# Evictions, clips and low parts in another order, a residual in transposing form, and a normalisation by single tiles at the end of an expert MLP kernel

## The reference

```python
q, k, v = x @ Wq, x @ Wk, x @ Wv
attn_out = softmax(q @ k.T * 512**-0.5) @ v @ Wp + bp
cms_out = gelu(attn_out @ cW1 + cb1) @ cW2 + cb2 + one_hot(code)
modifier = gelu(concat(attn_out, cms_out) @ mW1 + mb1) @ mW2 + mb2
x = clip(x + cms_out + modifier, 0, 1)                       # layer 0
h = gelu(x @ W_down[e] + b_down[e]) @ W_up[e] + b_up[e]      # layer 1, e per sequence
h = x + h
out = (h - mean(h)) * rsqrt(var(h) + 1e-5) * ln_w[e] + ln_b[e]
```

## Time and profile before

| | |
|---|---|
| three runs | 1076.14, 1076.20, 1076.23 us, median 1076.2 |
| the profiled execution | 1076.12 us, of which the span of the trace is 1074.3 us |
| PE busy | 1048.7 us, 98% of the span |
| DVE busy | 797.5 us, 74% |
| ACT busy | 516.6 us, 48% |
| granted clock of PE | 0.998 of full speed over the span |
| end of the last matmul, of the last DVE instruction | 1066.4 us, 1071.8 us |

### The profile page before, as it was taken

One profiled execution on the slowest core, in us unless ns is written; L12 is line 12 of the kernel. 1 busy time (PEld: TensorE's weight loads), 2 busy tenths in 40 slices (PEclk: granted clock), 3 DMA queues, 4 the chain that ended last, 5 costly groups with the idle time before them and its releaser, 6 DMA issues. The chain is left out here.

```text
span 1074.3 us, 13987 instructions
## 1 busy us (share of the span) xinstructions
PE 1048.7 (98%) x4986; PEld 874.4 (81%) x4986; DVE 797.5 (74%) x1394; ACT 516.6 (48%) x933; POOL 6.4 (1%) x15
## 2 busy tenths in 40 slices
PE   8999999999999999999999999999999999999997
PEld 7889778888877788888889877888887778888876
DVE  4436886776588888877675788677658888878786
ACT  4426755444264543433575485444425554343365
POOL 0000000000000000000000000000000000000001
PEclk9999999999999999999999999999999999999999
DMA  5600121210143242312753122312013323342152
GB/s 195 238 2 20 60 78 40 77 41 20 60 157 117 80 156 79 105 53 78 275 177 98 51 70 79 118 40 79 20 59 129 126 98 121 115 138 68 43 145 79
DMA packets 54718, 101.61 MB, mean 95 GB/s; under 512 B 3102, under 2 KB 31866, under 8 KB 50810
## 3 DMA queue, kind: packets, MB, share of 16 engines
q1 hardware_dynamic: 54560, 100.70, 27.0%
q10 hardware_dynamic: 90, 0.02, 0.0%
HBM read 79.74 MB, written 20.97 MB: 94 GB/s over the span
## 5 line engine op out<-in xcount | busy, mean ns | idle before, releaser
L1076 DVE TENSOR_TENSOR acc<-bank,acc 128x512 f32<-128x512 f32 x224 | 153.9, 687 | 84.9 <-PE bank L223 84.7
L221 PE MATMUL bank<-hid_hi,w_lo 128*128 128x512 f32 x512 | 200.5, 392 | 7.6 <-DVE hid_lo L965 4.7
L645 ACT ACTIVATE sbc<-sbc,bias 128x512 f32<-128x512 f32 x112 | 80.8, 724 | 254.8 <-DVE sbc L1046 193.4
L222 PE MATMUL bank<-hid_hi,w_hi 128*128 128x512 f32 x512 | 199.3, 389 | 0.0
L223 PE MATMUL bank<-hid_lo,w_hi 128*128 128x512 f32 x512 | 199.3, 389 | 0.0
L221 PE MATMUL bank<-ta_hi,w_lo 128*128 128x512 f32 x448 | 175.4, 392 | 2.5 <-ACT sbc L566 1.2
L223 PE MATMUL bank<-ta_lo,w_hi 128*128 128x512 f32 x448 | 174.4, 389 | 0.0
L222 PE MATMUL bank<-ta_hi,w_hi 128*128 128x512 f32 x448 | 174.3, 389 | 0.0
L1046 DVE TENSOR_TENSOR sbc<-bank,sbc 128x512 f32<-128x512 f32 x144 | 98.1, 686 | 42.6 <-PE bank L223 42.4
L221 PEld LDWEIGHTS bank<-hid_hi,w_lo 128*128 128x128 f32 x512 | 96.1, 188 | 31.8 <-DVE w_lo L965 3.6
L223 PEld LDWEIGHTS bank<-hid_lo,w_hi 128*128 128x128 f32 x512 | 96.1, 188 | 20.0
(11 more groups left out here) (223 smaller groups left out, 1556.4 us busy)
## 6 DMA issues: line engine op xcount, KB each, us to landing
w_raw<-in_L_cond_mW SPq DMA_DIRECT2D x48, 512.0 KB, 3.4
w_raw<-in_L_cond_cW SPq DMA_DIRECT2D x32, 512.0 KB, 4.3
pre_d<-sbc SPq DMA_DIRECT2D x10, 1024.0 KB, 3.9
sbc<-pre_d SPq DMA_DIRECT2D x10, 1024.0 KB, 7.2
x_raw<-in_x SPq DMA_DIRECT2D x4, 1024.0 KB, 6.2
e_raw<-in_L_cond_W_down SPq DMA_DIRECT2D x8, 512.0 KB, 5.2
e_raw<-in_L_cond_W_up SPq DMA_DIRECT2D x8, 512.0 KB, 4.4
out<-acc SPq DMA_DIRECT2D x16, 256.0 KB, 2.1
```

The lines of the kernel that those rows point to most:

```text
L221: nc.tensor.matmul(dst, w_l, a_h, start=start, stop=False, **kw)
L222: nc.tensor.matmul(dst, w_h, a_h, start=False, stop=False, **kw)
L645: nc.scalar.activation(dst, dst, ACT.Gelu, **kw).then_inc(g_done[key], 1)
L1076: nc.vector.tensor_tensor(dst, bank[:, :], dst, ALU.add).then_inc(evac, 1)
```

## The change

Four edits.

**The last round on DVE.** A new `dve_mlp_end` takes the last round of the last batch. Each of the four evictions of pair 2 is followed by the clip of its tile; each of the evictions 4 to 6, of pair 3, is followed by one low part of pair 2, and the fourth low part stands ahead of eviction 7. Pieces 4 and 5 (`e0l`) no longer stand among the evictions: piece 4 comes behind the clips of pair 3, and piece 5 behind the low parts of pair 3 (`dve_expert_last`).

The diff, cut to its core:

```diff
@@ pe_up
                     nc.tensor.matmul(ps[b0 + t][:, k * P:(k + 1) * P],
                                      acc[:, k, pp * TB + t * P:pp * TB + (t + 1) * P], ident[:, :],
-                                     start=k == 0, stop=True, skip_group_check=True)
+                                     is_transpose=True, start=k == 0, stop=True, skip_group_check=True)
@@ act_stats
+        A_STAT = ((0, 2), (0, 3), (1, 0), (1, 1), (1, 2))
+        def act_stats(act):
+            for c, (pp, t) in enumerate(A_STAT):
+                col = slice(TT * pp + t, TT * pp + t + 1)
+                bank = ps[(0 if pp else 4) + t][:, :]
+                act.wait_ge(up_mm, 4 * (2 * NBAT - 2 + pp) + t + 1)
...
@@ dve_norm_last
+            for t in (2, 3):
+                dve_eps_last(dve, 0, t)
+                dve_cent_last(dve, 0, t)
+                dve_out_last(dve, 0, t)
+            dve.wait_ge(z_done[0], 4 * bb + 4)
+            dve.wait_ge(ln_in[1], 64 * NBAT)
+            for t in (0, 1):
+                dve_eps_last(dve, 1, t)
+                dve_cent_last(dve, 1, t)
+                dve_out_last(dve, 1, t)
+            for t in (3, 2):
+                dve_eps_last(dve, 1, t)
+            for t in (2, 3):
+                dve_cent_last(dve, 1, t)
+            for t in (2, 3):
+                dve_out_last(dve, 1, t)
@@ the last round
+        def dve_mlp_end(dve, b):
+            i = QB - 1
+            dve_evac(dve, b, i - 1, 7)
+            dve_hid(dve, b, i, "12")
+            for k in range(KT):
+                dve_evac(dve, b, i, k)
+                dve_clip(dve, 2 * b, (k,))
+            for k in range(KT - 1):
+                dve_evac(dve, b, i, KT + k)
+                dve_xp(dve, 2 * b, (k,))
+            dve_xp(dve, 2 * b, (KT - 1,))
+            dve_evac(dve, b, i, 2 * KT - 1)
+            dve_clip(dve, 2 * b + 1)
+            dve_expert_piece(dve, b, 4)
@@ dve_expert_last
-            for k in (2, 3):
+            for k in (5, 2, 3):
                 dve_expert_piece(dve, bb, k)
...
-            dve_norm(dve, 2 * bb)
+            dve_norm(dve, 2 * bb, (0,))
```

More of the change, by code:

```diff
@@ L944, in act_expert_last @@
             act_up_bias(act, 2 * bb + 1)
[L945 to L956, removed]
+            act_stats(act)
+        A_STAT = ((0, 2), (0, 3), (1, 0), (1, 1), (1, 2))
+        A_NO = {pt: c for c, pt in enumerate(A_STAT)}
+        def act_stats(act):
[3 more added lines that the diff above has]
+                act.wait_ge(up_mm, 4 * (2 * NBAT - 2 + pp) + t + 1)
+                nc.scalar.activation(sjunk[:, c, 0, :], bank, ACT.Identity, accum_out=ssum[:, col]).then_inc(sum_done, 1)
+                act.wait_ge(sum_done, c + 1)
+                nc.scalar.activation(nmean[:, col], ssum[:, col], ACT.Copy, scale=-1.0 / V).then_inc(nmean_done, 1)
+                act.wait_ge(nmean_done, c + 1)
+                nc.scalar.activation(sjunk[:, c, 1, :], bank, ACT.Square, bias=nmean[:, col],
+                                     accum_out=ssq[:, col]).then_inc(ssq_done, 1)
         def act_program(act):
@@ L1118, in dve_resid, with dve_clip @@
             nc.vector.tensor_tensor(dst, dst, xf[:, t, :, :], ALU.add).then_inc(resid_done, 1)
-        def dve_clip(dve, n):
+        def dve_clip(dve, n, tiles=range(4)):
             b, t = divmod(n, 2)
-            for j in range(KT):
+            for j in tiles:
                 dve.wait_ge(evac, 8 * (RB * b + RB - 1) + KT * t + j + 1)
@@ L1165, in dve_expert_piece, with dve_xp @@
             sub(lo[:, s, :], e_raw[E_STAGE[bb][k]][:, s, :], hi[:, s, :]).then_inc(e_l, 1)
-        def dve_xp(dve, n):
+        def dve_xp(dve, n, tiles=range(4)):
             pp = n % 2
-            for j in range(KT):
+            for j in tiles:
                 dve.wait_ge(xp_h, 4 * n + j + 1)
@@ L1205, in dve_norm @@
                         .then_inc(z_done[pp], 1)
-        def dve_norm_last(dve):
[L1208 to L1225, removed]
@@ new lines, in build, with dve_eps_last @@
+        R_TILE = ((0, 2), (0, 3), (1, 0), (1, 1), (1, 3), (1, 2))
+        R_NO = {pt: 4 * NBAT - 3 + c + 1 for c, pt in enumerate(R_TILE)}
+        def dve_eps_last(dve, pp, t):
+            one = slice(t, t + 1)
+            if (pp, t) in A_NO:
+                col = slice(TT * pp + t, TT * pp + t + 1)
+                dve.wait_ge(ssq_done, A_NO[(pp, t)] + 1)
+                nc.vector.tensor_scalar(veps[:, one], ssq[:, col], 1.0 / V, LN_EPS, ALU.mult, ALU.add).then_inc(ve_done, 1)
+            else:
+                dve.wait_ge(up_mm, 8 * NBAT)
+                nc.vector.bn_stats(stat[:, t, :], ps[t][:, :]).then_inc(st_done, 1)
+                dve.wait_ge(st_done, 8 * NBAT - 5)
+                nc.vector.bn_aggr(mv[:, t, :], stat[:, t, :]).then_inc(ag_done, 1)
+                dve.wait_ge(ag_done, 8 * NBAT - 5)
+                nc.vector.tensor_scalar_add(veps[:, one], mv[:, t, 1:2], LN_EPS).then_inc(ve_done, 1)
@@ new lines, in dve_cent_last @@
+        def dve_cent_last(dve, pp, t):
+            n = 2 * NBAT - 2 + pp
+            mean = nmean[:, TT * pp + t:TT * pp + t + 1] if (pp, t) in A_NO else mv[:, t, 0:1]
+            nc.vector.scalar_tensor_tensor(out=z_tile(pp, t), in0=ps[(0 if pp else 4) + t][:, :], scalar=mean,
+                                           in1=ln_p[n][:, t // TS, 0, :],
+                                           op0=ALU.add if (pp, t) in A_NO else ALU.subtract, op1=ALU.mult)\
+                .then_inc(z_cent, 1)
@@ new lines, in dve_out_last @@
+        def dve_out_last(dve, pp, t):
+            n = 2 * NBAT - 2 + pp
+            dve.wait_ge(rstd_done, R_NO[(pp, t)])
+            dve.wait_ge(z_cent, 4 * n + t + 1)
+            nc.vector.scalar_tensor_tensor(out=z_tile(pp, t), in0=z_tile(pp, t), scalar=rstd[:, t:t + 1],
+                                           in1=ln_p[n][:, t // TS, 1, :], op0=ALU.mult, op1=ALU.add)\
+                .then_inc(z_done[pp], 1)
+        def dve_norm_last(dve):
+            bb = NBAT - 1
+            for t in (2, 3):
[14 more added lines that the diff above has]
+                dve_out_last(dve, 1, t)
@@ L1419, in dve_mlp @@
                 if it >= QB and b + 1 == NBAT:
-                    dve_expert_piece(dve, b, 1 if it == QB else 5)
-                last = it == QB + 1 and b + 1 == NBAT
+                    dve_expert_piece(dve, b, 1)
                 turn = it == QB + 1 and b + 1 < NBAT
-                if last:
-                    dve_clip(dve, 2 * b)
                 down(4)
@@ L1437, in dve_mlp @@
                 down(6)
[L1438 to L1441, removed]
+            dve_clip(dve, 2 * b)
             dve_evac(dve, b, QB - 1, 7)
@@ L1470, in pool_program @@
             pool.wait_ge(consts, 1)
+            halves = [slice(2 * h, 2 * h + 2) for h in range(2)]
+            singles = [slice(t, t + 1) for t in range(TT)]
             for n in range(NB):
-                for h in range(2):
-                    part = slice(2 * h, 2 * h + 2)
-                    pool.wait_ge(ve_done, 2 * n + h + 1)
+                last = (halves[0], singles[2], singles[3]) if n == NB - 2 else tuple(singles[t] for t in (0, 1, 3, 2))
+                for c, part in enumerate(halves if n < NB - 2 else last):
+                    pool.wait_ge(ve_done, (2 * n if n < NB - 1 else 2 * NB - 1) + c + 1)
                     nc.gpsimd.tensor_tensor(rstd[:, part], veps[:, part], mhalf[:, part], ALU.pow).then_inc(rstd_done, 1)
```

13 lines of the change are left out of this document (8 added, 5 removed).

## The result

| | before | after |
|---|---|---|
| median (lowest to highest) | 1076.22 us (1076.14 to 1076.48, 4 runs) | 1065.78 us (1065.63 to 1065.96, 4 runs) |
| ratio, 95% interval | | 0.9902, 0.989 to 0.9913 |
| the profiled execution, its span | 1076.12, 1074.3 us | 1065.9, 1064.0 us |
| granted clock of PE over the span | 0.998 | 0.999 |
| end of the last matmul, of the last DVE instruction | 1066.39, 1071.78 us | 1056.65, 1061.44 us |

The kernel is 10.4 us faster. 3.05 were forecast: 1073.1 us, in a range from 1072.1 to 1074.7. The first table of the page of after, to be read against the earlier trace rows, says where to look: PE has 64 instructions fewer (4986 before) and 8.7 us less to do (1048.7 before), though no edit takes a product out of the program.

What follows compares the result with a forecast made beforehand. PE, busy for 98% of the span, was taken to bound the kernel. Terms of -2.3, -0.7, +0.5, -0.3 and -0.25 sum to -3.05 us against 1076.12, giving 1073.1 us; 8-in-10 range 1072.1 to 1074.7.

Steps and rivals of the forecast that it cites:

- (4): Residual's matmuls in transposing form on PE: slightly smaller spacing per instruction, 0.3 us gained in all, between 0 and 0.34.
- (1): Last round: with DVE's new order no group waits for DVE and `pe_down` starts at 1033.6; 2.3 us gained.
- (2): First 12 matmuls of `pe_down`: pair 2's low parts are ready in time, so no waiting; 0.7 us gained.
- (3): Pair 3's down product: PE waits for the moved piece 5; 0.5 us lost, bounds 0 and 1.0.
- (5): Tail behind PE's last matmul: single-tile normalisation with statistics on ACT and DVE, 5.39 to 5.15 us; 0.25 us gained.
- A: Rival: DVE falls behind in the interleaved last round and holds PE, losing 1.5 us of gain; 1074.6 us, chance 0.13.
- B: Rival: single tiles in the tail cost more than they save, each unit waiting for POOL; 1073.9 us, chance 0.08.
- D: Rival: DVE's pieces come before PE wants them and POOL's one-column power takes half; 1072.1 us, chance 0.07.
- C: Rival: PE's clock falls during 32 transposes, slowing the up products behind them; 1078.5 us, chance 0.05.

Runs made afterwards that it cites:

- e1: Kernel before with only the transposing flag on the residual's 64 matmuls; 1068.65 us, ratio 0.9931.
- e2: Changed kernel with the residual's flag taken back, so plain matmuls again; 1073.39 us, ratio 0.9972.
- e5: Kernel before, residual of pairs 2 and 3 as plain product on fp32r operands, without bias and low part; 1072.93 us, ratio 0.9966.
- e6: Kernel before with the 32 transposes of the attention weights as plain float32 products with the identity; 1079.69 us, ratio 1.0031.
- e7: Kernel before with the transposing flag on the residual of pairs 2 and 3 only; 1072.6 us, ratio 0.9963.
- e3: Kernel before with only the last round's new order on DVE, pieces 4 and 5 moved behind the evictions; 1073.61 us, ratio 0.9976.
- e4: Kernel before with only the normalisation edits: single tiles, statistics on two engines; 1075.54 us, ratio 0.9993.
- e0: Changed kernel run once more, unaltered; 1065.68 us.
- e9: Changed kernel with POOL making piece 4's low part only behind pair 2's clips, DVE making piece 5 behind pair 3's clips; 1066.53 us.
- e8: Changed kernel with POOL instead of DVE making the low parts of pieces 4 and 5, right behind their high parts; 1067.2 us.

## Why the prediction was wrong, point by point

**(4), the transposing form, is the term that failed.** It was put at 0.3 us and measured at 7.1 to 7.7. The step took the spacing of one instruction of each form (0.109 and 0.112 us, both right) and multiplied their difference by the rows' 32, as if the form could change only the duration of one and not how many there are. Sixteen products at 2 x 0.109 us before (3.49/32), 16 at 0.104 (1.66/16) after: the price of a product halved. The prediction's own sign for this step was a row of L449 x32 of 3.66 us; the trace has x16 of 1.91. It could have been read without a run. The earlier trace rows show x32 for L449 and x16 for L360; the text of the kernel has 4 x 4 products in the one and 4 x 4 transposes in the other. The section on the kernel even says "32 float32 matmuls of 128 columns a pair", which is the count of the trace put in place of that of the code. e1 (one line, 7.7 us), e2 (3.0 us without it), e5 (fp32r, no flag, the same 16 instructions) and e6 (the reverse, 3.4 us slower) show that the count is the cause. Of the two places each gives its half (e7).

The Trainium skill's page "FP8 and Floating Point Precision", section "TensorE Precision Notes", says that true float32 takes four passes through the array. The trace shows two instructions for a product in place of one; how many passes each makes no run here shows. By that rule a factor would have been asked of the flag rather than a difference: as an estimate from the page, and if the transposing form takes a single pass, three quarters of 3.49 us for each of four pairs, 10.5 us. The trace shows about half, 7.3.

**(1) and (2)** came to 0.02 us as forecast, and e3 alone gives them. **(3)**, the new wait for piece 5, was 0.47 by the adding up and 0.44 in the trace, released by `e0l` as named, 7.5 us behind the first matmul of `pe_down` (forecast 7.4); the row's idle time alone is 0.17, less than the 0.3 to 0.4 named as the sign, and the slow start is the rest.

**(5), the tail, was right in its mechanism and too small**: 0.60 us for 0.25. The duration for a power on one column, taken at 0.69 for want of a row, is 0.55. Only pair 3 lies in the tail: DVE is through with pair 2 and idles 0.80 us before 1054.47. The prediction had two units of 1.65 us and then results that wait 0.2 us for POOL's last two powers. In the trace the units take 1.59 and 1.58 (1054.47 to 1056.06 to 1057.64), and the last results start at 1060.03, right behind the centrings, as POOL's two powers were over by 1059.85. That is 0.13 and 0.2 of the 0.35 us. By times alone e4 can't tell the gain from none.

**Rivals.** A and B would have made the forecast worse and did not come: no group waits for DVE, and single tiles save. D did not come either: the power on one column takes 0.55 us, four fifths of 0.69 and not half, and the loss of (3) stayed. C did not come: the products behind 16 transposes start 0.227 us apart. The granted clock, 0.999, says less, as it reads 1.00 in every microsecond from 3 to 8 of before too, where the transposes of `wq_raw` take 421 ns. The Trainium skill's rule in "TensorE: Matmul & The Clock Gate", section "Part 4: PE-mode transpose" (full clock does not engage for transposes) is not borne out by this case, with 0.227 us between those products and with transposes that fall from 421 to 272 ns among themselves. Rival C's 32 in a row never arise, for the same reason for which (4) failed: they are 16. What 32 would do no run here shows.

Do the parts add up? e1, e3 and e4 give 7.7 + 2.7 + 0.8 = 11.2 us by their medians, the whole change 10.4 to 10.7. The medians of the parts are each uncertain by a few tenths, and the 0.5 to 0.8 between them isn't explained here. The second batch's share of (4) is 3.45 us in the table, against 2 x 1.83 = 3.66 by the rows of a pair. The two views of line 449 say why: the first residual starts at 551.5 us before and at 551.8 after, so after was some 0.3 us late ahead of anything that the change edits (the same start lies between 551.2 and 551.6 in e0, e1, e2 and e3), and from there on it gains 3.7.

## What to carry to other kernels

Before pricing a change of form, put the count of rows that a line has in the trace beside the count that the code makes. Where they differ by a factor, look for a form or a type without it before pricing one instruction: here the factor was two, and the flag was worth half of the line, not the difference of two durations. And before giving work to an idle engine, ask what memory it reads while its neighbour works: moving a use later in a queue cost nothing here, where moving the work to POOL lost more than the wait was worth.

## What the runs showed of the hardware

- A plain product with float32 operands (128 x 128 by 128 columns) is two instructions on PE, 0.218 us for both, and a load of weights for each of 192 ns (before, e2, e6); in transposing form one, 0.104 to 0.109 us, with a load of 140 ns (after, e1). As a plain product on fp32r operands it is one too, 0.109 us, but the load stays at 192 ns (e5). The view of e2's line 449 has the first form, as that of before has:

```profile
L449 PEld LDWEIGHTS bank<-ident,acc x128: 187/192/193, 551.4 to 1057.9; 128*128 128x128 f32 x128
```

- POOL's subtraction on 128 x 1024 in SBUF takes 2.4 us in e9 and 2.6 and 2.8 in e8, and DVE's instructions that read only SBUF are held up meanwhile: a clip from 0.43 to 1.53 and 1.84 us, a low part from 0.68 to 2.29, the 1.84 and the 2.29 ending 0.3 and 0.5 us after POOL. Those that read a PSUM bank beside SBUF keep their 0.75. The Trainium skill says this in "SBUF — State Buffer", section "Who interferes with whom": one pair of ports is shared by the two engines and held for a whole instruction; an instruction of VectorE with two SBUF inputs meets GpSimd's reads there, one with a single SBUF input does so only in a mode that uses both port pairs (`tensor_scalar`, the clip's operation, can enter such a mode), and any other stays clear. The trace agrees for the low part (2.29 for 0.68) and the eviction (0.75), and for the clip (1.84 for 0.43) if it ran in such a mode, which no row names. The forecasts of e8 and e9 left this out; the rivals recorded beside them had it.
- A power on one column takes POOL 0.55 us and on two 0.69: the second column adds 0.14, so most of the 0.55 does not come from the column.
- The granted clock of a stretch can read 1.00 while PE runs at half pace. From 3 to 8 us of before it does, and the first eight transposes, 1.94 us in all and 0.421 each, start (1.94 - 0.42)/7 = 0.217 us apart, twice the 0.109 of those in the earlier trace rows. The spacing of like matmuls shows the pace.
